# One score buffer of two PSUM banks instead of two of one, and one exponential for two heads

## The reference

```python
    def _L1_xattn_ref(query, key, value, Wq, Wk, Wv, Wo):
        q = (query @ Wq).reshape(b, sq, NUM_HEADS, HEAD_DIM).transpose(0, 2, 1, 3)
        k = (key @ Wk).reshape(b, sk, NUM_KV_HEADS, HEAD_DIM).transpose(0, 2, 1, 3)
        v = (value @ Wv).reshape(b, sk, NUM_KV_HEADS, HEAD_DIM).transpose(0, 2, 1, 3)
        k = jnp.repeat(k, rep, axis=1)
        v = jnp.repeat(v, rep, axis=1)
        scale = HEAD_DIM ** (-0.5)
        scores = jnp.einsum('bhqd,bhkd->bhqk', q, k) * scale
        probs = jax.nn.softmax(scores, axis=-1)
        out = jnp.einsum('bhqk,bhkd->bhqd', probs, v)
        out = out.transpose(0, 2, 1, 3).reshape(b, sq, DIM)
        return out @ Wo
```

## Time and profile before

| | us |
|---|---|
| median of 3 runs | 1009.19 (1008.36 to 1012.31) |
| profiled execution, its own time | 1010.14 |
| its span, first to last instruction | 1008.3 |
| PE busy | 923.8 (92%) |
| VectorE (DVE) busy | 687.5 (68%) |
| GpSimd (POOL) busy | 499.4 (50%) |
| ScalarE (ACT) busy | 435.3 (43%) |
| the 512 exponentials (L692) | 277.9, 595 ns each |
| mean granted TensorE clock | 0.973 |

### The profile page before, as it was taken

One profiled execution on the slowest core, in us unless ns is written; L12 is line 12 of the kernel. 1 busy time (PEld: TensorE's weight loads), 2 busy tenths in 40 slices (PEclk: granted clock), 3 DMA queues, 4 the chain that ended last, 5 costly groups with the idle time before them and its releaser, 6 DMA issues.

```text
span 1008.3 us, 16862 instructions
## 1 busy us (share of the span) xinstructions
PE 923.8 (92%) x5232; PEld 371.1 (37%) x5232; DVE 687.5 (68%) x982; ACT 435.3 (43%) x746; POOL 499.4 (50%) x204
## 2 busy tenths in 40 slices
PE   3988899868889987999999999999999998999998
PEld 2665665323445433222222222222222221444443
DVE  4788867999865698777777777777777740345532
ACT  3333324422312233566666666666666666012110
POOL 5232255584400244466777767666777778201200
PEclk9999999879999998899999999999999999999999
DMA  5854202021021432111111000001111000000011
GB/s 179 326 168 146 72 33 64 1 67 59 1 96 58 133 116 73 29 30 30 31 29 27 5 26 29 29 29 29 29 29 30 1 1 1 1 1 0 21 71 75
DMA packets 38904, 54.83 MB, mean 54 GB/s; under 512 B 7504, under 2 KB 27984, under 8 KB 38864
## 3 DMA queue, kind: packets, MB, share of 16 engines
q1 hardware_dynamic: 38864, 54.28, 16.4%
HBM read 41.55 MB, written 12.58 MB: 54 GB/s over the span
## 4 chain that ended last, share of the span: by engine, by line
PE 68%; DVE 17%; DVEq 5%; issue 4%; ACT 2%; DMA 1%; POOLq 1%; SPq 0%; POOL 0%; ACTq 0%
PE sbank L1414 12%; PE sbank L1405 12%; PE mpair L1349 10%; PE sbank L1424 6%; DVEq L752 5%; PE sbank L1195 3%; PE sbank L1196 3%; PE sbank L1197 3%; PE sbank L1497 3%; PE sbank L1523 3%; PE sbank L1501 3%; PE sbank L1499 3%; PE sbank L1525 3%; DVE mx L1041 2%; DVE r L1028 1%
## 5 line engine op out<-in xcount | busy, mean ns | idle before, releaser
L1041 DVE TENSOR_REDUCE mx<-mpair 128x1 f32<-128x1024 f32 (+1 forms) x256 | 307.2, 1220 | 105.8 <-PE mpair L1349 102.3
L692 ACT ACTIVATE regC<-sbank 128x512 f32<-128x512 f32 x512 | 277.9, 595 | 146.7 <-PE sbank L1405 144.2
L464 POOL TENSOR_TENSOR regD<-regC 128x2048 f32<-128x2048 f32 x32 | 145.3, 4539 | 60.9 <-ACT regC L692 60.9
L1405 PE MATMUL sbank<-regD 98*128 98x512 f16 x512 | 161.8, 388 | 5.3 <-ACT regC L692 2.9
L464 POOL TENSOR_TENSOR wraw<-regC 128x2048 f32<-128x2048 f32 x32 | 145.1, 4534 | 38.2 <-ACT regC L692 38.2
L1349 PE MATMUL mpair<-regD 96*128 96x512 f16 x512 | 149.5, 388 | 9.1 <-DVE mx L1041 6.1
L1414 PE MATMUL sbank<-regC,regD 128*32 128x512 f32 x1024 | 136.4, 605 | 1.0 <-ACT regC L692 1.0
L1405 PEld LDWEIGHTS sbank<-regD 98*128 98x128 f16 x512 | 37.1, 97 | 203.6 <-ACT regC L692 183.2
L1349 PEld LDWEIGHTS mpair<-regD 96*128 96x128 f16 (+1 forms) x512 | 49.0, 99 | 68.9 <-DVE mx L1041 13.9
L413 POOL TENSOR_SCALAR wraw<-wraw 128x1024 f32<-128x1024 f32 x16 | 17.7, 1103 | 94.4 <-ACT regR L625 86.7
L488 POOL TENSOR_TENSOR kq_hi<-y,r 128x1024 f16<-128x1024 f32 x8 | 17.0, 2126 | 84.7 <-ACT r L731 84.7
(11 more groups left out here) (164 smaller groups left out, 1426.2 us busy)
## 6 DMA issues: line engine op xcount, KB each, us to landing
xT_lo<-in_ctx SPq DMA_DIRECT2D x16, 512.0 KB, 5.9
wraw<-in_L_ffn_W_int SPq DMA_DIRECT2D x8, 512.0 KB, 6.8
wraw<-in_L_xattn_Wq SPq DMA_DIRECT2D x8, 512.0 KB, 3.3
regD<-q_hi_scratch SPq DMA_DIRECT2D x32, 128.0 KB, 2.4
wraw<-in_L_xattn_Wo SPq DMA_DIRECT2D x8, 512.0 KB, 3.3
out<-X SPq DMA_DIRECT2D x16, 256.0 KB, 2.0
X<-in_x SPq DMA_DIRECT2D x2, 1024.0 KB, 9.0
X<-in_x SPq DMA_DIRECT2D x1, 2048.0 KB, 14.1
```

Source lines behind the costliest of these rows:

```text
L464: nc.gpsimd.tensor_tensor(p_sum[pr % 2][:, :, :], probs[:, (2 * pr) % 4, :, :], probs[:, (2 * pr) % 4 + 1, :, :], ALU.add).then_inc(s["p_a ...
L692: nc.scalar.activation(probs[:, kt % 4, h, :], bank[4 + h % 2], ACT.Exp, scale=SCALE).then_inc(s["exp_ok"], 1)
L1041: v.tensor_reduce(mx[m][:, bass.ds(n, 1)] if par is not None else mx[m][:, n:n + 1], slot[:, :, :], AX.XY, ALU.max).then_inc(s["mx_red"], 1)
L1405: pe.matmul(bank[4 + h % 2], kst[par][0:98, kt * P:(kt + 1) * P], qst[par][0:98, h * 512:(h + 1) * 512], start=True, stop=True).then_inc(s ...
```

## The change

Banks 4 and 5 become one tensor `spair` of two banks; `sbank` keeps two, for the numbers 6 and 7. The exponential takes both banks of the pair at once (`exp_pair`), 1024 wide, into the same two heads of the ring's slot, and adds 2 to `exp_ok`. It waits until both scores are there. On PE both scores of a pair wait until the previous pair's exponential is done. `acc_out` stands after the first pair of the first key tile, where it stood before.

```diff
         mpair = [ctx.enter_context(nc.psum_tensor(f"mpair{i}", [P, 2, 512], F32)) for i in range(2)]
-        sbank = [ctx.enter_context(nc.psum_tensor(f"sbank{i}", [P, 512], F32)) for i in range(4)]
+        spair = ctx.enter_context(nc.psum_tensor("spair", [P, 2, 512], F32))
+        sbank = [ctx.enter_context(nc.psum_tensor(f"sbank{i}", [P, 512], F32)) for i in range(2)]
         bank = [mpair[0][:, 0, :], mpair[0][:, 1, :], mpair[1][:, 0, :], mpair[1][:, 1, :],
-                sbank[0][:, :], sbank[1][:, :], sbank[2][:, :], sbank[3][:, :]]
+                spair[:, 0, :], spair[:, 1, :], sbank[0][:, :], sbank[1][:, :]]
...
-            def exps(g, kt, h, first):
+            def exp_pair(g, kt, side, first):
-                act.wait_ge(s["st_mm"], 32 * g + 4 * kt + h + 1)
-                if h == 0 and not (first and kt < 4):
+                act.wait_ge(s["st_mm"], 32 * g + 4 * kt + 2 * side + 2)
+                if side == 0 and not (first and kt < 4):
                     act.wait_ge(s["pv_mm"], KT * g + kt - 3)
                     act.wait_ge(s["p_add"], NPAIR * g + kt // 2 - 1)
-                nc.scalar.activation(probs[:, kt % 4, h, :], bank[4 + h % 2], ACT.Exp,
-                                     scale=SCALE).then_inc(s["exp_ok"], 1)
+                nc.scalar.activation(probs[:, kt % 4, 2 * side:2 * side + 2, :], spair[:, :, :], ACT.Exp,
+                                     scale=SCALE).then_inc(s["exp_ok"], 2)
...
                 for kt in range(KT):
-                    for h in range(REP):
-                        exps(g, kt, h, first)
-                        if kt == 0 and h == 1 and not first:
+                    for side in range(2):
+                        exp_pair(g, kt, side, first)
+                        if kt == 0 and side == 0 and not first:
                             acc_out(g - 1)
...
                 for h in hs:
                     if not (first and kt == 0 and h < 2):
-                        pe.wait_ge(s["exp_ok"], 32 * g + 4 * kt + h - 1)
+                        pe.wait_ge(s["exp_ok"], 32 * g + 4 * kt + 2 * (h // 2))
                     pe.matmul(bank[4 + h % 2], kst[par][0:98, kt * P:(kt + 1) * P],
```

## The result

The changed kernel takes 1053.72 us (median of four runs, 1053.48 to 1056.91) against 1009.21; the ratio is 1.0447, 95% interval 1.0422 to 1.0472. It is slower by some 45 us. The forecast was 1046 in a range of 1037 to 1062.

The account below looks back on a forecast made before the run. PE was taken to bound the attention stage. Longer turns add 26.5 us in thirteen middle groups, 3.0 in group 14, 4.3 in group 15, 3.3 in the first: 37.1 together, forecast 1046 us, range 1037 to 1062.

Parts of the forecast that it names:

- The bound and the direction: Attention stage: PE bounds, ScalarE's saved 15 us is worth nothing, longer turns between score pairs make the kernel 3.7% slower.
- The exponential: ScalarE's 1024 wide exponential takes 1.02 us, taken from a 1024 wide f16 copy out of PSUM; bounds 1.02 and 1.19.
- ScalarE to PE: Hand-over from an exponential's end to the next score's weight load on PE: 0.06 us.
- PE to ScalarE: From a pair's first matmul to its exponential: 0.56 or 0.42 us by heads, plus 0.22 for the second score.
- to either comes the second score: The exponential now waits for the pair's second score, adding 0.22 us to either start distance.
- The 0.14 for the slot waits: Exponential of heads 0 and 1 starts 0.14 us later, put down to two waits for the probabilities' slot.
- VectorE's wait: Middle group's 2.58 us interval: scores start 0.42 later, covering PE's 0.40 us wait for VectorE, leaving 2.17.
- The covered intervals: Eight intervals of 1.97 us per middle group stay unchanged, with 0.11 to 0.24 us to spare.
- rival (a): Attention stage: if the exponential costs 1.19 us, the 1.97 intervals of heads 0 and 1 lengthen too; 1069 us, chance 0.08.
- rival (b): Last group: waits of over 1 us could halve PE's clock, up to +15 us, 1061; chance 0.05.
- (c): Attention stage: exponential and both hand-overs in 1.3 us or less, nearly all hidden, waits saved; 999 us, chance 0.02.
- (d): Attention stage: PE's waits all absorbed by something that waits later anyway, no difference; 1009 us, chance 0.02.

Follow-up runs that it names:

- PE's wait alone: Kernel before, but both scores of a pair wait on PE until both previous exponentials are done, exponentials 512 wide; 1028.0 us, ratio 1.0190.
- ScalarE's alone: Kernel before, but both 512 wide exponentials wait for the pair's second score, PE as before; 1030.8 us, ratio 1.0225.
- the shorter exponential: Changed kernel with the exponential over only the first 256 queries of each of the two banks; 1011.3 us, ratio 1.0025.
- counted in pairs: Changed kernel with the exponential adding 1 instead of 2 to exp_ok and every wait on it halved; 1047.6 us, ratio 1.0383.
- the flat access: Changed kernel with the two banks and two heads each written as one flat row of 1024 in the exponential; 1054.0 us, ratio 1.0455.
- Both waits narrow: Kernel before with the changed kernel's waits on PE and ScalarE, but two 512 wide exponentials in sequence; 1057.3 us, ratio 1.0473.
- the slot waits first: Changed kernel with ScalarE's two waits for the probabilities' slot put ahead of its wait for the scores; 1047.3 us, ratio 1.0389.
- three quarters: Changed kernel with the exponential over 384 queries of each bank, the last quarter left out; 1029.6 us, ratio 1.0214.
- the swap: Kernel before with probabilities times V of the group before put ahead of the maxima item in key tile 0; 1000.2 us, ratio 0.9918.

## Why the prediction was right, and what was off

**The bound and the direction** held. PE bounds the stage, the exponential's 15 us less on ScalarE brought nothing, and the single buffer put a turn of scores, exponential and two hand-overs between any two pairs. That this turn is the cause is shown from four sides: PE's wait alone costs near its computed price, in the time and in the intervals (ScalarE's alone in the time, by other intervals than computed), both together without the wide exponential cost the whole, the shorter exponential takes the loss away, and each small delay removed from the turn shortens the time by about what was worked out for it.

**The exponential** at 1.02 us, read from a copy of another type, was right: 1.024. The Trainium skill ("ScalarE: Activation LUTs", What ACT_TABLE_LOAD costs) gave 1.04, an estimate from its figures; the measurement decides.

**ScalarE to PE**, 0.06 us, held: 476.84 plus 1.02 ends at 477.86, the next scores start at 477.92.

**PE to ScalarE** was the mis-sized term: 0.64 us forecast after heads 2 and 3, measured 0.70. The step "to either comes the second score" was right by itself, as the kernel with both waits and narrow exponentials shows (0.64). The 0.06 comes from an edit that the prediction passed over without a price, the increment by 2. So the turns were 1.78 and 1.88 to 1.93 instead of 1.73 and 1.86. In a middle group that is four turns by 0.05 and three by 0.02 to 0.07: a group of 30.71 instead of 30.43. With the increment by 1 the group is 30.40 and the time 1047.6, beside a forecast of 1046. The forecast of the time was 7.7 us short. In the profile it was 6.5 (43.6 for 37.1): 3.6 in the middle groups, which the increment accounts for, and 3.5 in the three others, less the 0.6 by which the stage began earlier. The median of the kernel counted in pairs is 6 us nearer, but its profile is also without the 1.1 us of the clock's dip below. Against the profile with the flat access, which has no dip there either, it is 0.30 shorter in each middle group and 0.4 and 0.7 in the last two, so some 5 us are shown to be the increment's.

**The 0.14 for the slot waits** held as a cause. As a size it held in key tiles 0, 4 and 6 (0.85 against 0.70); it was 0.10 in 1, 2, 5 and 7, and nothing in 3. The forecast read it from one pair of a middle group and one of the last, and took it for all key tiles.

**VectorE's wait** came out near the number, 2.12 for a forecast of 2.17, partly by luck. The forecast took the wait as 0.40 and all of it as covered; by the starts it was about 0.6, of which 0.14 is left.

**The covered intervals**, rival (a), did not open: 1.97 in every middle group, since the longest turn was 1.93. They had 0.04 us to spare, less than the 0.11 claimed.

**The clock**, rival (b), came in small. From 860.2 to 864.3 us the granted clock was 0.58, mostly at the 1.2 GHz level, after 4.2 us in which PE was busy for 2.75. Two intervals of group 14 (859.59 to 862.07 to 864.36) became 2.48 and 2.29 instead of 1.93 and 1.78: 1.1 us. In the last group, where I had looked for it, it stayed at 1.00. Both waits narrow shows such a dip at the same place (0.55 and 0.60 in 862 to 864 and 864 to 866 us) and a second one in the last group; the change with the slot waits first, with the flat access and counted in pairs show 1.00 from 840 to 890 us, so it isn't fixed to the place. In three quarters the clock fell only after the last scores (0.70 in 880 to 885 us). The Trainium skill's account of brief idles that make the clock go up and down ("TensorE: Matmul & The Clock Gate", A second HAM failure mode) would fit the dip of group 14, and not the middle groups, which stayed at 1.00 with waits of 0.2 to 0.7 us in them.

**The other groups** were 14.1 us together, 10.6 forecast: 4.7, 4.4 and 5.0 instead of 3.3, 3.0 and 4.3. In the first group the half clock put up the first two intervals to 2.24 and 2.21 as expected, but the stretch at the lower clock went on (0.50 from 411 to 413 us, where the kernel before had 1.00), and the third interval took 3.68 us instead of 2.61, with one probabilities-times-V of 1.93 us instead of 1.06 in it. Key tile 2 of the first group has no row sums, so an interval of 1.07 became 1.78 there, where the middle groups' went from 1.58 to 1.88. Group 14 has the dip in it, group 15 fifteen times the 0.05.

**Faster or no difference**, (c) and (d): nothing bore them out in the change. The wait for VectorE that (c) named was real, and the swap turned it into 7 to 8 us.

## What to carry to other kernels

Joining two buffers into one to make an instruction larger saves its fixed cost only on an engine that bounds; what it costs is the overlap, and the price can be worked out beforehand: write down the shortest turn (producer, hand-over, consumer, hand-over) and hold it against each interval in which the producing engine has other work. Here PE's own work was shorter than the turn in 7 of 16 intervals; six of them grew, and the seventh (1.92, now 1.93) had held a wait of its own before. On such a turn put waits that are met early ahead of the one that ends last, and try a semaphore that counts by one: here the two were worth some 6 us each, tried apart.

## What the runs showed of the hardware that I had not expected

- An activation that adds 2 to a semaphore starts 0.06 us later than one that adds 1, everything else the same (0.70 against 0.64 us after the first score, on heads 2 and 3; 0.80 to 0.85 against 0.78 to 0.80 on heads 0 and 1; 1054.0, with the flat access, against 1047.6 us for the kernel).
- Two waits already met, placed behind the one that ends last on ScalarE, cost 0.10 to 0.15 us of latency in seven of eight key tiles, some 6 us in the changed kernel.
- A 1024 wide exponential over two banks (1.02 us) is only 0.06 shorter than two of 512 in sequence (1.08 to 1.09), since these overlap by 0.1.
- The idle time printed before the maxima item understates its wait here, since it counts from the modelled end of the record before: PE's 0.40 for VectorE was about 0.6 by the starts, and moving the item behind a microsecond of other work gave back 0.56.
